# First batch of a decoder layer: ScalarE gets the constant casts and eight DMA issues, four engines get a new order of units

## The reference

```python
kv_c = x @ W_kv                                   # 64 latents, RMS-normed, times g_kv
q_c = x @ W_q                                     # 128 latents
k_content, v, q_content = heads(kv_c @ W_kdec), heads(kv_c @ W_vdec), heads(q_c @ W_qdec)   # 16 heads x 16
k_rope, q_rope = rope(heads(x @ W_krope)), rope(heads(q_c @ W_qrope))                       # 16 heads x 32
scores = concat(q_content, q_rope) @ concat(k_content, k_rope).T * scale, causal
x = layernorm(x + softmax(scores) @ v @ W_o)
x = layernorm(x + cross_attention(x, ctx_1024) @ W.T + b)
x = layernorm(x + experts(x))                     # top 2 of 8, gelu between two matmuls
```

## Time and profile before

| | us |
|---|---|
| median of 3 runs | 674.92 |
| lowest and highest | 674.2, 677.16 |
| the profiled execution | 680.18 |
| its span | 678.1 |
| TensorE busy in it | 598.3 |
| VectorE busy in it | 522.6 |
| ScalarE busy in it | 407.5 |
| GpSimd busy in it | 297.0 |

### The profile page before, as it was taken

How to read it: one execution, slowest core, us unless ns; L and a number is a source line. 1 busy time by engine, 2 the same in 40 slices (tenths; PEclk the granted TensorE clock), 3 DMA queues, 4 the chain that set the end, 5 groups by cost and what they waited for, 6 DMA issues and landing times.

```text
span 678.1 us, 21310 instructions
## 1 busy us (share of the span) xinstructions
PE 598.3 (88%) x7553; PEld 441.7 (65%) x7553; DVE 522.6 (77%) x1106; ACT 407.5 (60%) x874; POOL 297.0 (44%) x247
## 2 busy tenths in 40 slices
...
GB/s 280 100 144 96 110 135 116 67 128 105 66 94 99 67 57 37 91 2 161 107 163 136 0 66 114 133 26 48 42 42 57 54 50 48 49 49 50 126 71 139
DMA packets 39921, 59.76 MB, mean 88 GB/s; under 512 B 6832, under 2 KB 27568, under 8 KB 39696
## 3 DMA queue, kind: packets, MB, share of 16 engines
...
## 4 chain that ended last, share of the span: by engine, by line
PE 62%; DVE 14%; issue 14%; ACT 4%; POOL 3%; DMA 2%; SPq 1%; ACTq 0%; DVEq 0%; POOLq 0%
PE bank L1805 9%; PE bank L1807 5%; PE bank L1395 4%; PE bank L1421 3%; PE scores L1795 3%; DVE mx L1134 3%; PE bank L1374 3%; PE scores L1797 3%; PE scores L1796 3%; PE scores L1452 3%; DVE mxc L1169 3%; PE bank L1795 2%; PE bank L1797 2%; PE bank L1796 2%; PE bank L1375 2%
## 5 line engine op out<-in xcount | busy, mean ns | idle before, releaser
L786 ACT ACTIVATE probs<-scores 128x768 f32<-128x768 f32 (+1 forms) x128 | 114.6, 917 | 50.2 <-PE scores L1428 32.6
L661 POOL DMA_INDIRECT acc_rows<-x,slot_row x39 | 65.0, 1666 | 108.4 <-DVE x L1301 97.6
L1805 PE MATMUL bank<-w_sb,wp 128*128 x312 | 109.8, 379 | 1.4 <-DVE wp L1288 1.3
L1169 DVE TENSOR_REDUCE mxc<-scores 128x4 f32<-128x1024 f32 x64 | 76.2, 1218 | 15.3 <-PE scores L1468 14.8
L1807 PE MATMUL bank<-w_sb,wp 128*128 x312 | 85.0, 273 | 0.0
L857 ACT ACTIVATE probs<-scores,b_sb 128x128 f32<-128x128 f32 x160 | 45.5, 368 | 56.9 <-PE scores L1797 55.5
L857 ACT ACTIVATE probs<-bank,b_sb 128x128 f32<-128x128 f32 x152 | 43.5, 369 | 52.0 <-PE bank L1797 52.0
L1286 DVE CAST wp<-probs 128x512 f16<-128x512 f32 x78 | 34.6, 444 | 50.7 <-ACT probs L857 49.5
L595 POOL TENSOR_TENSOR rstd<-rstd,minus_half 128x2 f32<-128x2 f32 x16 | 14.1, 879 | 127.0 <-DVE rstd L939 127.0
L1134 DVE TENSOR_REDUCE mx<-scores 128x6 f32<-128x768 f32 x64 | 59.6, 951 | 7.3 <-PE scores L1428 6.6
L1795 PE MATMUL scores<-xT,w_sb 128*128 128x128 f16 x320 | 61.5, 225 | 3.3 <-DVE xT L977 3.3
...
## 6 DMA issues: line engine op xcount, KB each, us to landing
...
wstage<-in_w_exp SPq DMA_DIRECT2D x16, 512.0 KB, 4.2
w_sb<-in_w_exp SPq DMA_DIRECT2D x8, 512.0 KB, 4.0
wp<-in_w_exp SPq DMA_DIRECT2D x8, 512.0 KB, 3.4
x_sb<-in_x_by_feature SPq DMA_DIRECT2D x8, 256.0 KB, 4.3
ctx_raw<-in_ctx SPq DMA_DIRECT2D x8, 256.0 KB, 3.0
x_res<-in_x SPq DMA_DIRECT2D x8, 256.0 KB, 3.5
x_rows<-x SPq DMA_DIRECT2D x8, 256.0 KB, 2.5
```

The source lines that it names most:

```text
L661: nc.gpsimd.indirect_dma_start(out=acc_rows[:, :], out_offset=bass.IndirectOffsetOnAxis(ap=slot_row[:, n:n + 1], axis=0), in_=yb[n % 2], i ...
L786: nc.scalar.activation(probs[:, 2 * (k % 4):2 * (k % 4) + 2, 0:cols], ps_p[pair[u, k, b]][:, :, 0:cols], ACT.Exp, scale=(SELF_SCALE, CROSS ...
L1169: nc.vector.tensor_reduce(mxc[:, 2 * k:2 * k + 2, :], ps_p[pair[u, k, b]][:, :, :].rearrange("p h (a k) -> p h a k", a=2), axis=AX.X, op=A ...
L1805: mm(o[:, 0:2 * D], ah[:, u, f, :], weights(e, at, 2 * D), start=(f == 0), stop=(f == FC - 1), skip_group_check=True)
```

## The change

Nothing is computed otherwise. Five things are moved, all in batch 0; TensorE's list is the same word for word.

- `ph1` and `pl1` go up one or two places, to before the latents' units.
- The five mask casts leave VectorE for ScalarE, as `mk.0` after the second weight piece's high half. VectorE waits for `c_ld` at its first maximum instead.
- The eight `mc.0` are issued from ScalarE's DMA queue. The moves of the batches 1 to 7 stay on SyncE.
- SyncE's list loses these eight, and what is left of batch 0 closes up: the third weight piece and the first of the next batch come earlier among the rope moves, `x.3` comes after the last rope move and not before the middle ones.
- GpSimd does `lo2.0` and `lo3.0` directly after their `ad`, ahead of `xl.2` and `cx.0`.

```diff
 SCALAR_ORDER = """
-ph0.0 xt.0 sq.0 qc.0 ph1.0 wh0.0 xt.1 ph2.0 wh1.0 ca0.0 ca1.0 wh2.0 ct0.0 ct1.0 sq.1 xt.2 qc.1 cx.0 ca2.0 ca3.0 wh3.0
+ph0.0 xt.0 ph1.0 sq.0 qc.0 wh0.0 xt.1 ph2.0 wh1.0 mk.0 ca0.0 ca1.0 wh2.0 ct0.0 ct1.0 sq.1 xt.2 qc.1 mc0.0 mc1.0 mc2.0
+cx.0 ca2.0 mc3.0 mc4.0 ca3.0 mc5.0 mc6.0 mc7.0 wh3.0 xt.3 va.0 ca0.1 ca1.1 ct0.1 vc.0 sq.2 qc.2 wh0.1 ct1.1 se0.0
...
 VECTOR_ORDER = """
-pl0.0 kv.0 la.0 pl1.0 wl0.0 ro0.0 ro1.0 ro2.0 kt.0 pl2.0 ro3.0 wl1.0 ct0.0 ct1.0 kv.1 wl2.0 la.1 mk.0 kt.1 ro0.1 ro1.1
+pl0.0 pl1.0 kv.0 la.0 wl0.0 ro0.0 ro1.0 ro2.0 kt.0 pl2.0 ro3.0 wl1.0 ct0.0 ct1.0 kv.1 wl2.0 la.1 kt.1 ro0.1 ro1.1
...
 GPSIMD_ORDER = """
-xl.0 lr.0 xl.1 ro0.0 ad0.0 ro1.0 ad1.0 lo0.0 ro2.0 ro3.0 lo1.0 lr.1 ad2.0 ad3.0 xl.2 lo2.0 cx.0 lo3.0 ro0.1 ro1.1
+xl.0 lr.0 xl.1 ro0.0 ad0.0 ro1.0 ad1.0 lo0.0 ro2.0 ro3.0 lo1.0 lr.1 ad2.0 lo2.0 ad3.0 lo3.0 xl.2 cx.0 ro0.1 ro1.1
...
 SYNC_ORDER = """
-rl0.0 rl1.0 x.0 w0.0 rl2.0 w1.0 c.0 rl3.0 x.1 rl4.0 x.2 w2.0 mv0.0 mv1.0 mc0.0 r.0 mc1.0 mc2.0 mc3.0 w3.0 mv2.0 mc4.0
-w0.1 mc5.0 mc6.0 x.3 mv3.0 mv4.0 mv5.0 mv6.0 mv7.0 mc7.0 mc0.1 mc1.1 mv0.1 w1.1 mc2.1 mv1.1 w2.1 x.4 mv2.1 mv3.1 mv4.1
+rl0.0 rl1.0 x.0 w0.0 rl2.0 w1.0 c.0 rl3.0 x.1 rl4.0 x.2 w2.0 mv0.0 mv1.0 r.0 w3.0 mv2.0 mv3.0 w0.1 mv4.0 mv5.0 mv6.0
+mv7.0 x.3 mc0.1 mc1.1 mv0.1 w1.1 mc2.1 mv1.1 w2.1 x.4 mv2.1 mv3.1 mv4.1 mc3.1 mc4.1 mc5.1 mv5.1 mv6.1 mc6.1 mc7.1
...
+                elif u == "masks":
+                    act_e.wait_ge(t_ld, 32)
+                    act_e.wait_ge(c_ld, 16 * len(const_loads[4]))
+                    nc.scalar.activation(ident_b[:, :], ident, ACT.Copy)
+                    nc.scalar.activation(ident_h[:, :], ident, ACT.Copy)
+                    nc.scalar.activation(mask_b[:, :, :].rearrange("p a m -> p (a m)"), raw_masks[:, M_QUERY:M_QUERY + 2 * QK], ACT.Copy)
+                    nc.scalar.activation(half_b[:, :, :, :].rearrange("p s a m -> p (s a m)"), raw_masks[:, M_HALF:M_HALF + 4 * P], ACT.Copy)
+                    nc.scalar.activation(up_b[:, :], raw_masks[:, M_UP:M_UP + P], ACT.Copy).then_inc(c_bf, 1)
+                elif u == "move_content":
+                    act_e.wait_ge(v_ct, b * 2 + k // 4 + 1)
+                    row = 2 * HD * (k % 4)
+                    nc.scalar.dma_start(qk16[QK - HD:QK + HD, k, :, :], cont16[row:row + 2 * HD, k // 4, :, :]).then_inc(c_mv[k], 16)
...
-                elif u == "masks":
-                    dve.wait_ge(t_ld, 32)
-                    dve.wait_ge(c_ld, 16 * len(const_loads[4]))
-                    nc.vector.tensor_copy(ident_b[:, :], ident)
...
                 elif u == "self_max":
+                    if b == 0 and k == 0:
+                        dve.wait_ge(c_ld, 16 * len(const_loads[4]))
                     dve.wait_ge(pe_max[0], b * (H // 2) + k + 1)
```

More of the change, by code:

```diff
@@ new lines @@
+cx.0 ca2.0 mc3.0 mc4.0 ca3.0 mc5.0 mc6.0 mc7.0 wh3.0 xt.3 va.0 ca0.1 ca1.1 ct0.1 vc.0 sq.2 qc.2 wh0.1 ct1.1 se0.0
+se1.0 se2.0 ca2.1 ca3.1 se3.0 se4.0 wh1.1 sv0.0 se5.0 se6.0 se7.0 sv1.0 sv2.0 wh2.1 sv3.0 xt.4 ca0.2 ca1.2 ca2.2 sb.0
+va.1 ca3.2 sq.3 ct0.2 qc.3 se0.1 se1.1 ss.0 ct1.2 se2.1 se3.1 st0.0 st1.0 wh3.1 st2.0 se4.1 st3.0 se5.1 sv0.1 wh0.2
+se6.1 se7.1 sv1.1 sv2.1 sv3.1 ca0.3 ca1.3 cx.1 wh1.2 sb.1 va.2 wh2.2 xt.5 ce0.0 ce1.0 ce2.0 ce3.0 ct0.3 cv0.0 ce4.0
+sq.4 ss.1 qc.4 ce5.0 ce6.0 cv1.0 cv2.0 ce7.0 ca2.3 st0.1 st1.1 cv3.0 ca3.3 wh3.2 st2.1 st3.1 se0.2 se1.2 se2.2 vc.1
```

33 lines of the change are left out of this document (21 added, 12 removed).

## The result

The changed kernel takes 666.45 us in the median of 4 runs (666.15 to 670.57), the kernel before 676.04 (674.2 to 681.49) beside it: ratio 0.988, 95% interval 0.9835 to 0.9924. I had forecast 671.2. Two later comparisons of the same two programs gave 0.9934 (0.9908 to 0.996) and 0.9938 (0.991 to 0.9965), that is 4.2 to 4.5 us. So there are two questions: is my 3.7 us the right mechanism, and where do the 8.1 us by the ratio (0.012 of 676; the two medians lie 9.6 apart) come from.

The account below looks back on a forecast made before the run. The start was taken as bound by a chain through all engines, the rest by TensorE's work. The later of two paths put `kv.2` at 51.5 to 52.0 against 55.40; 3.7 us off 674.92 gave 671.2 us, range 669.5 to 674.7.

Parts of the forecast that it names:

- passes TensorE's full stretch whole: Behind `kv.2`, batches 0 and 1 keep their distances and the 3.7 us gain reaches the end undiminished.
- 0.05 in the chances: Chance given to a larger gain, with the clock rising sooner and GpSimd's gaps shorter.
- The rope start: Rope weights split earlier, in idle time of ScalarE and VectorE: TensorE starts at 14.02 instead of 15.70, 1.68 us sooner.
- The carry to batch 1's latents: From rope start to batch 1's latents the whole 1.68 us carries: TensorE at 33.55 instead of 35.23.
- the clock as a rival: Second scores of batches 0 and 1 meet 7.4 us more at half speed, cancelling the gain: 674.9 us; chance 0.14.
- The casts: Five mask casts in ScalarE's idle time, 18.1 to 19.8, 1.7 us, `ca0.0` at 20.36; 5.24 us taken from VectorE.
- The issues on ScalarE: Each content-move issue from ScalarE's queue costs 0.62 us, priced by SyncE's; first two begin at 31.4 and 32.0.
- The rival's mechanism: ScalarE and SyncE take turns issuing, 1.2 us each: `kv.2` at 53.3, gain 2.1, 672.8 us; chance 0.18.
- A list held up by 1.85 an issue: Issues delay ScalarE's list, `ca2.0` and `kv.2`: gain gone at 1.85 us each, 678.3 us from 3.0; chance 0.08.
- Latents to the first maximum: Batch 1's latents at 33.55, `kt.1` ends at 36.1, scores no longer await casts, maxima begin at 42.9 to 44.5.
- my better case: TensorE's clock rises at about 38.5, so maxima begin at 42.9 rather than 44.5, `kv.2` at 50.4 by that path.
- The post: `kv.2`, where all engines' lists meet: through GpSimd's `ad1.1` at 49.1 plus 2.4, not before 51.5, against 55.40.

Follow-up runs that it names:

- e10: The changed kernel with the five mask casts back on VectorE, ahead of `kt.1`: 672.46 us beside 675.33 of before, ratio 0.9934.
- e11: The changed kernel with the content moves back on SyncE and SyncE's and GpSimd's old orders: 672.47 us beside 675.33 of before, ratio 0.9926.
- e15: The changed kernel run once more, unaltered, for its third profile: 670.55 us beside 675.02 of before, ratio 0.9938.
- e8: The kernel before run once more, unaltered, for a second profile: 676.82 us beside 677.06 of before, ratio 0.998.
- e9: The kernel before with only GpSimd's order changed (`lo2.0` ahead of `ad3.0`, `xl.2` behind `lo3.0`): 674.22 us, ratio 0.9973 to before.
- e13: The changed kernel with GpSimd's order alone put back, moves still on ScalarE: 670.29 us beside 675.02 of before, ratio 0.9928.
- e14: The same kernel as e11, run again beside the changed kernel on one chip: 669.96 us beside 675.02 of before, ratio 0.9914.
- e3: The kernel before with only the content moves on ScalarE's queue and SyncE's and GpSimd's new orders: 673.11 us beside 676.59, ratio 0.9955.
- e4: The changed kernel run once more, unaltered, for its second profile: 670.99 us beside 676.59 of before, ratio 0.9934.
- e5: The changed kernel with 138 dummy matmuls in TensorE's waits up to 50 us, plus ten later: 672.08 us beside 677.06 of before, ratio 0.9906.
- e7: As e5, with more dummy matmuls in the waits of the last two batches and the gate: 672.17 us beside 677.06 of before, ratio 0.9907.

## Why the prediction was right and wrong

**Which steps failed.** Two, each by taking something as the same in every execution: the first TensorE's clock at the start, the second the time of the long part. At the start I carried "the whole 1.68" to batch 1's latents, and the profile shows 3.17 (35.23 to 32.06). Behind the start I wrote that the gain "passes TensorE's full stretch whole", and in the profile it grew from 7.05 at 340 us to 12.6 at 460. A clock that helps had no term in the sum and, with shorter gaps of GpSimd, 0.05 in the chances. What follows goes along the sum, and comes to the second step at the end.

**The rope start: right.** I forecast 14.02 for TensorE's first rope matmul and 1.68 sooner. Measured: 14.28, and 1.57 once the landing of x (7.44 against 7.29) is taken out (1.59 at VectorE's first rotation). Both halves lay in idle time as costed.

**The carry to batch 1's latents: the first step that failed.** I carried "the whole 1.68: TensorE at 33.55"; it was 32.06. Three of the weights-first kernels show what I meant: 25.79 to 25.88 (e10, e11, e15) against 27.47, that is 1.6 to 1.7. Five others, the first profile among them, stand at 24.1 to 24.2, another 1.7 sooner. TensorE's timelines of the changed kernel's second and third profile, at the same instruction, tell the two apart:

```profile
26.53 0.27 PE L1379 MATMUL bank<-xT,wp 128*128 128x256 f16 x1
26.64 0.27 PE L1380 MATMUL bank<-xT,wp 128*128 128x256 f16 x1
```

```profile
29.72 0.40 PE L1379 MATMUL bank<-xT,wp 128*128 128x256 f16 x1
29.91 0.42 PE L1380 MATMUL bank<-xT,wp 128*128 128x256 f16 x1
```

One starts 0.11 behind the other at 2.4 GHz, and 0.2 at 1.2 GHz. In the second profile the clock was low from 22.0 to 25.4, in the third from 24.6 to 31.4, so that the same program met batch 0's content projections and batch 1's latents at one level or the other. Before was low from 24.5 to 31.4, its other profile (e8) only from 24.4 to 27.8. Counted from ScalarE's first copy of x, TensorE's starts in the second and the third profile agree to within 0.1 us up to 11.3, and they part inside `qk2.0`, whose matmuls then take 0.27 in one and 0.42 in the other: the clock first rose at 18.6 and at 21.2, which is 11.3 and 12.7 behind that copy. Nothing but the clock differs first. My chain took one of two outcomes of before for a constant. I had the clock as a rival, but only as one that takes the gain back.

**The casts: right.** Forecast 18.1 to 19.8 at 1.7 us, and `ca0.0` at 20.4; measured 17.80 to 19.22, 1.4 us, and 20.60. The Trainium skill's rule that I had weighed (page Perfetto Trace Analysis, section Optimizing Scalar/DVE Operations: VectorE's fast mode is faster) is right by e9, where VectorE needs 1.25 for the five against ScalarE's 1.42; I was wrong to say that the trace disagrees with it; what made its 5.24 was GpSimd beside it, and the row of 1.17 against 0.51 that I quoted said so. I priced the removal and missed that the new GpSimd order removes the same wait.

**The issues on ScalarE: the price was right; the turns exist and cost little.** Taken at 0.62; measured in the first profile 0.61, 0.62, 0.58 and 0.60 each (1.24 for two, 1.16 for two, 1.80 for three), the first of them while `xt.2` ran, and others while SyncE issued rope moves of its own (four from 29.40, 0.61 each). But single issues are longer where both queues are at it. In e15 two that start 0.02 apart on ScalarE and SyncE take twice the usual 0.59, both of them:

```profile
32.43 1.17 ACTq L734 DMA_DIRECT2D w_sb<-w_sb  x1
32.45 1.16 SPq L524 DMA_DIRECT2D w_sb<-w_sb  x1
```

In the first profile SyncE's issue at 27.39, during which ScalarE's first begins, takes 1.20. That agrees with the Trainium skill's rule of one lock on the generator (page Perfetto Trace Analysis, section DMA Instruction — HWDGE), though before has one issue of 1.33 with no second queue, so not every long one is a turn. The rival's mechanism is thus there, but its price is not: it wanted three issues of 1.2 ahead of `ca2.0`, e15 has one of 1.17 and stands 0.26 behind the first profile on the way from latents to `kv.2`, and e13 with the issues on ScalarE is as fast there as e14 without. A list held up by 1.85 an issue is out. What I had too small was the landing: the first three took 3.5 to 5.3 us against my 4.6 at worst. Since they were issued from 28.02 and not from 31.4, `mc1.0` was there at 33.94, before its scores at 34.88.

**Latents to the first maximum: mis-sized.** I had 2.55 us to the end of `kt.1`'s matmuls and then 6.8 to 8.4 to the maximum; the part behind `kt.1` took 6.1 to 6.2 us in nine profiles, since TensorE's clock had risen by 35.56, and 7.0 in e3 and e10, where it stayed low until about 41. That is 0.7 shorter than my better case, and 1.5 shorter than in before (7.6), where the clock was low until 45.0.

**The post: right in kind.** I said that GpSimd and ScalarE would bound `kv.2`, with `ad1.1` to 49.1 and the post 2.4 behind. `ad1.1` ended at 46.94, `kv.2` began 2.24 behind it and waited 0.96. `x.3`, forecast for 46.4, was there at 43.3 and bounded nothing.

**The sum.** Where the clock was alike in both programs up to batch 1's latents, low from about 24.5 to 31.4 (before and e15), the post is 48.10 - 43.67 = 4.43 sooner; by terms 1.65 at the latents, 2.5 up to `kt.1`, 1.5 up to the maximum, and -1.26 between maximum and post, together 4.4. With e8 and the first profile after, it is 4.86. At 300 us the same pairs are 5.2 and 5.1 apart, and the two larger comparisons measured 4.5 and 4.2. So the mechanism's worth is 4 to 5 us where I said 3.7, inside the range. That my number came near is in part luck: I had the part behind `kt.1` too long, and did not see that GpSimd's new order costs 1 us at the post.

**The rest of the 8.1 us: the second step that failed.** The growth between 340 and 460 us is not the change's, for the kernel before shows it too when it runs again:

| us sooner than the first profile of before | at 340 us | at 460 us | at 1.2 GHz between |
|---|---|---|---|
| before | 0 | 0 | 34.1 |
| e8, before again | 1.2 | 3.7 | 23.9 |
| changed | 7.05 | 12.6 | 17.1 |
| e4, changed again | 7.5 | 9.9 | 27.3 |
| e15, changed, third | 4.0 | 7.1 | 23.9 |
| e5, changed, waits filled | 6.7 | 6.7 | 34.1 |
| e7, also late waits filled | 2.9 | 5.8 | 13.7 |

Except in e7, the gain in this stretch goes with the time at 1.2 GHz, about 0.3 us for each us less. It goes so in the times too. In the first comparison three of the changed kernel's four runs had a mean clock of 0.971 and took 666.2 to 666.8; the fourth had 0.960 and took 670.6. In the next two comparisons the mean over its 10 and 12 runs was 0.962 and 0.961, against 0.959 of before. Over all runs of this study a line through span and time at 1.2 GHz, with each kernel its own level, gives 0.26 us per us; a mean clock of 0.971 in place of 0.961 is 2 x 0.010 x 667 = 13 us less at half speed, 3.4 us by that line. So e4 answers what it was run for: the first profile contains luck, 3.8 us of span.

That the clock is the cause here, and not a sign of waits that differ for another reason, is argued and not shown: e7 took 20 us of low time out of this stretch against e5 and gained 2.9 in it, 0.14 per us, and nothing in its time. Whether the first comparison's four runs were chance, or something on that chip favoured the changed program, stays open as well.
